# A prologue of layer norm and weight splitting, put in another order

## The chip, the core and the metric

The kernel runs on one core of a Trainium2 chip. The metric is the device time of one execution, in microseconds. Lower is better. The median of three runs of the kernel before is 1116.12 us (1115.36 to 1117.17).

## The reference

One transformer layer: cross attention, then a feed-forward network with quantised operands. Cut to what matters here, with shapes:

```python
# x (32, 100, 256), ctx (32, 361, 256), WQ, WK, WV (16, 256, 64), WO (1024, 256)
xn = (x - mean(x)) / sqrt(var(x) + 1e-5)            # over the last axis
Qh = einsum('btd,hdk->bhtk', xn, WQ)                 # 16 heads of 64
Kh = einsum('btd,hdk->bhtk', ctx, WK); Vh = einsum('btd,hdv->bhtv', ctx, WV)
attn = softmax(Qh Kh^T / sqrt(64) + mask * -1e9)
x = x + concat(attn Vh) @ WO
y = (x - mean(x)) / sqrt(var(x) + 1e-5)
x = x + qlinear(gelu(qlinear(y, W1, b1)), W2, b2)    # affine 8-bit codes of the input, symmetric of the weight
```

## The kernel before, in words

The kernel is written engine by engine: each of the five engines has its own instruction list in program order, and semaphores alone connect them. Nothing reorders it. An instruction that waits holds up everything behind it on its engine.

Phase 1, where the change lies, makes the query projection for all 32 batch rows, before a loop over the 32 rows does the attention. It goes through `NB` = 8 chunks of `TB` = 4 batch rows, 400 tokens each (`TW`). For chunk c:

- SyncE loads x into `xs` (`load_x`, L480), and between the chunks the four weights WQ, WK, WV, WO (L477 and L490), all through one queue.
- VectorE takes `bn_stats` of the four rows (`stats_x`, L876). Mean and variance follow from the two halves of each statistic by eight small operations (`ln_moments`, L461 to L468), each waiting for the one before. VectorE does them for chunk 0, GpSimd for the others. GpSimd then computes `rstd` by a power (L566) and `shift` (L567).
- ScalarE writes the normalised `xn` (`norm_x`, L685), TensorE transposes it (`x_transposes`, L1183), ScalarE copies the transposes out as f16 `xnT_h` (`x_high`, L693), and VectorE subtracts to get the remainder `xnT_l` (`x_low`, L881). Every operand is thus a high and a low f16 part.
- A weight is split likewise. VectorE takes the absolute maximum per partition (`abs_w`, L839), TensorE transposes it (`top_w`, L1191), VectorE makes the unit and its inverse (`unit_w`, L845 to L849), ScalarE writes the high part (`high_w`, L677) and VectorE the low part (`low_w`, L869), each in two halves of 512 columns.
- TensorE multiplies (`q_chunk`, calling `split3`, L366 to L368): eight products m of 400 columns, each the sum over two halves k of the contraction of high x high, high x low and low x high. Even m go to the PSUM bank `proj[0]`, which ScalarE copies out (`q_out`, L697), odd m to `proj[1]`, which VectorE copies out (`q_out`, L886). In the middle of a chunk, before m = 4, TensorE transposes the next chunk.

In VectorE's order, work for later chunks and weights stands between the copies. Before the first copy, at L945 to L956, stand the statistics of chunks 0, 1 and 2 and the whole preparation of WQ. On ScalarE the normalisation of chunk 1 stands ahead of the first copy, and on TensorE the transposes of chunk 0 stand ahead of WQ's `top_w`.

Of the kernel before, what the change touches and what calls it, by code (L numbers as in the profile page):

```python
# [15 lines left out]
F32 = mybir.dt.float32  # L16
# [4 lines left out]
ALU = mybir.AluOpType  # L21
# [155 lines left out]
def build(nc, x, ctxT, mask, wq, wk, wv, wo, w1T, b1, w2T, b2, out):  # L177
# [5 lines left out]
    def place(name, shape, dt, at=None):  # L183
        size = {F32: 4, F32R: 4, BF16: 2, F16: 2}[dt]
        n = size
        for d in shape[1:]:
            n *= d
        if at is None:
            at = cursor[0]
            cursor[0] = (at + n + 31) // 32 * 32  # L190
            assert cursor[0] <= top, (name, cursor[0], top)
        return nc.alloc_sbuf_tensor_at(name, shape, dt, offset=at)
# [10 lines left out]
    stats = place("stats", [P, B, 6], F32)  # L203
    mean = place("mean", [P, B], F32)
    var = place("var", [P, B], F32)
    rstd = place("rstd", [P, B], F32)
    shift = place("shift", [P, B], F32)
    lnt = place("lnt", [P, 4, B], F32)
# [161 lines left out]
    def wait(eng, s, n):  # L370

        eng.wait_ge(s, n + CREDIT)
# [6 lines left out]
    def chain(eng, s):  # L379

        count = [0]

        def link(ins):
            count[0] += 1
            ins.then_inc(s, 1)
            eng.wait_ge(s, count[0])
        return link
# [157 lines left out]
    def _(pool):  # L545
# [12 lines left out]
        link = chain(pool, s_lp)  # L558
        for c in range(NB):
            bs = slice(c * TB, (c + 1) * TB)  # L560
            if c == 0:
                pool.wait_ge(s_lv, 8)
            else:
                pool.wait_ge(s_st, TB * (c + 1))
                ln_moments(link, pool, c)
            link(pool.tensor_tensor(rstd[0:T, bs], var[0:T, bs], mhalf[0:T, bs], ALU.pow))  # L566
            pool.tensor_tensor(shift[0:T, bs], mean[0:T, bs], rstd[0:T, bs], ALU.mult).then_inc(s_rs, 1)  # L567
# [103 lines left out]
    def _(act):  # L671
# [8 lines left out]
        def norm_x(c, par):  # L680

            act.wait_ge(s_rs, c + 1)
            for i in range(TB):
                b = c * TB + i
                ins = act.activation(xn[0:T, par, i, :], xs[0:T, b, :], ACT.Identity, scale=rstd[0:T, b:b + 1],  # L685
                                     bias=shift[0:T, b:b + 1])
            ins.then_inc(s_xn, 1)
# [7 lines left out]
        def q_out(c, m):  # L695
            act.wait_ge(s_qp, NM * c + m + 1)
            act.activation(q_slot[:, c * TB:(c + 1) * TB, m, :], proj[0][:, 0:TW].rearrange("p (b t) -> p b t", b=TB),  # L697
                           ACT.Copy, scale=QS).then_inc(s_qe[0], 1)

        def q_chunk(c, par, more=True):  # L700
            split = (c - 1 if 2 <= c <= 4 else None)
            q_out(c, 0)
            if split:
                high_w(split, 0)
            q_out(c, 2)
            if more:
                x_high(c + 1, 1 - par)
            q_out(c, 4)
            if c + 2 < NB:
                norm_x(c + 2, par)  # L710
            if c == NB - 2:
                act.wait_ge(s_msk, 16)
                act.activation(mask_b[0:T, 0:S], mask_b[0:T, 0:S], ACT.Copy, scale=-1.0e9).then_inc(s_mb, 1)
            if split:
                high_w(split, 1)
            q_out(c, 6)
# [1 line left out]
        x_high(0, 0)  # L718
        high_w(0, 0)
        high_w(0, 1)  # L720
        norm_x(1, 1)
        for c in range(NB - 1):
            if c == NB - 2:
                act.wait_ge(s_wlo, 8)
# [107 lines left out]
    def _(dve):  # L832
# [39 lines left out]
        def stats_x(c):  # L872

            dve.wait_ge(s_x[c], 16)
            for b in range(c * TB, (c + 1) * TB):
                dve.bn_stats(stats[0:T, b, :], xs[0:T, b, :]).then_inc(s_st, 1)  # L876
# [29 lines left out]
        def q_chunk(c, par, more=2):  # L906

            q_out(c, 1)
            if c < 3:
                abs_w(c + 1, 0)  # L910
            elif c < 6:
                low_w(c - 2, 0)
            else:
                abs_f(3 * (c - 6))
            q_out(c, 3)
            if more:
                x_low(c + 1, 1 - par)
            q_out(c, 5)
            if more == 2 and c + 3 < NB:
                stats_x(c + 3)  # L920
            if 1 <= c <= 3:
                unit_w(c)
            if c == 6:
                abs_f(1)
            if c == 7:
                unit_f()
            q_out(c, 7)
            if c < 3:
                abs_w(c + 1, 1)
            elif c < 6:  # L930
                low_w(c - 2, 1)
            elif c == 6:
                abs_f(2)
            if c == 4:
                ctx_max(0)
            if c == 5:
                wait(dve, s_ct, 1)
                ctx_top(0, tp[0])
                dve.scalar_tensor_tensor(out=wconst[:, 0:1], in0=wunit[:, 0:1], scalar=GS, in1=wunit[:, 1:2],
                                         op0=ALU.mult, op1=ALU.mult).then_inc(s_wc, 1)  # L940
                dve.wait_ge(s_wc, 1)
                ctx_unit(0)
                dve.scalar_tensor_tensor(out=wconst[:, 1:2], in0=wunit[:, 2:3], scalar=1.0 / VS, in1=wunit[:, 3:4],
                                         op0=ALU.mult, op1=ALU.mult).then_inc(s_wc, 1)
        stats_x(0)  # L945
        dve.wait_ge(s_st, TB)
        ln_moments(chain(dve, s_lv), dve, 0)
        stats_x(1)
        abs_w(0, 0)
        abs_w(0, 1)  # L950
        unit_w(0)
        low_w(0, 0)
        start(dve, (s_k, s_v, s_cm, s_cr, s_sv, s_max, s_mg, s_hv, s_ri, s_nrm, s_x1, s_ln))
        x_low(0, 0)
        low_w(0, 1)
        stats_x(2)  # L956
        for c in range(NB):
# [215 lines left out]
    def _(pe):  # L1173
# [28 lines left out]
        def top_ctx(a, ps):  # L1202
            wait(pe, s_cm, a + 1)
            pe.transpose(ps[:, 512 - P:512], cmax[:, 0:1].broadcast_to([P, P]), ident[:, :]).then_inc(s_ct, 1)

        def q_chunk(c, par, more=True):
            wait(pe, s_xtl, KD * (c + 1))
            for m in range(NM):
                if m == NM // 2 and more:
                    x_transposes(c + 1, 1 - par)  # L1210
                if m == NM // 2 and 1 <= c <= 3:
                    top_w(c)
                if m == NM // 2 and c == 5:
                    top_ctx(0, tp[0])
                if m == NM // 2 and c == NB - 1:
                    top_f()
                wait(pe, s_qe[m % 2], NM // 2 * c + m // 2)
                if c == 0 and m % (NM // 2) == 0:
                    pe.wait_ge(s_wlo, m // (NM // 2) + 1)
                for k in range(KD):  # L1220
                    ms = slice(m * P, (m + 1) * P)
                    ins = split3(pe, proj[m % 2][:, 0:TW], (wq_h[:, k, ms], wq_l[:, k, ms]),
                                 (xnT_h[:, par, k, :], xnT_l[:, par, k, :]), k == 0, k == KD - 1)
                ins.then_inc(s_qp, 1)
        x_transposes(0, 0)
        top_w(0)
        for c in range(NB):
            q_chunk(c, c % 2, c < NB - 1)

# [219 lines left out]
```

## Time and profile before

| | |
|---|---|
| median of three runs | 1116.12 us |
| the profiled execution | 1116.15 us |
| its span in the trace | 1114.3 us |
| TensorE matmul busy | 1026.3 us (92%) |
| VectorE busy | 982.0 us (88%) |
| ScalarE busy | 866.6 us (78%) |
| GpSimd busy | 770.5 us (69%) |

The span is what the trace covers, from the first instruction to the last, and the time of the execution holds 1.85 us more. Busy shares are averages over the whole program. In the first of forty slices (28 us each) TensorE is busy 4 tenths, and 9 tenths in nearly all others. In the rows below, PE is TensorE's matmuls, PEld its weight loads, DVE VectorE, ACT ScalarE, POOL GpSimd, and SPq SyncE's queue.

### The profile page before, as it was taken

How to read it: one execution, taken by the hardware profiler on the slowest of the kernel's cores; microseconds unless marked ns; L12 is line 12 of the kernel's file. 1: busy time of each engine (PE TensorE's matmuls, PEld its weight loads, DVE VectorE, ACT ScalarE, POOL GpSimd, SP SyncE). 2: the span in 40 equal slices, each digit the busy share in tenths (PEclk: the TensorE clock that was granted, in tenths of full speed). 3: DMA queues.
4: the chain of work that ended last, by engine and by line, in shares of the span. 5: the costliest groups of instructions: out<-in, count | busy, mean ns of one | idle time of the engine just before them, and what ended most of it. 6: DMA issues, size and time to landing. Idle time of an engine off the chain costs nothing.

```text
span 1114.3 us, 37739 instructions
## 1 busy us (share of the span) xinstructions
PE 1026.3 (92%) x10639; PEld 649.0 (58%) x10639; DVE 982.0 (88%) x2538; ACT 866.6 (78%) x1809; POOL 770.5 (69%) x1106
## 2 busy tenths in 40 slices
PE   4999999999999999999999999999999999998828
PEld 2555566666666666666666666666666666665317
DVE  5776999999999999999999999999999999996997
ACT  4555888888888888888888888888888888886906
POOL 2337777777777777777777777777777777774800
PEclk9999999999999999999999999999999999999969
DMA  8301665555555555555555555555555555554003
GB/s 260 109 1 29 130 131 136 136 132 132 131 129 135 136 136 136 134 129 133 136 133 129 134 132 129 135 136 129 128 135 136 135 131 129 132 136 143 1 0 119
DMA packets 435437, 136.77 MB, mean 123 GB/s; under 512 B 407666, under 2 KB 434390, under 8 KB 435414
## 3 DMA queue, kind: packets, MB, share of 16 engines
q1 hardware_dynamic: 435414, 136.47, 51.0%
q8 instruction: 13, 0.21, 0.1%
q14 instruction: 10, 0.08, 0.0%
HBM read 28.60 MB, written 6.55 MB: 32 GB/s over the span
## 4 chain that ended last, share of the span: by engine, by line
PE 75%; DVE 10%; ACT 6%; issue 4%; POOL 3%; DVEq 1%; DMA 1%; ACTq 1%; SPq 0%; POOLq 0%
PE front L366 19%; PE front L368 17%; PE front L367 17%; PE back L1300 8%; PE front L1278 6%; PE tp L1278 5%; POOL hl L610 3%; DVE hrange L1129 2%; DVE hrange L1130 2%; DVE prob L979 2%; ACT prob L736 2%; DVE k_l L1028 1%; ACT q_h L790 1%; ACT ctx_h L786 1%; PE front L1415 1%
## 5 line engine op out<-in xcount | busy, mean ns | idle before, releaser
L610 POOL TENSOR_TENSOR hl<-prob,hl 100x361 f16<-100x361 f32 x511 | 432.0, 855 | 96.6 <-DVE hl L986 50.7
L736 ACT ACTIVATE prob<-prob,nmax 100x361 f32<-100x361 f32 x512 | 293.8, 586 | 47.7 <-DVE nmax L979 47.6
L366 PE MATMUL front<-ctx_h,wk_h 128*128 128x362 f16 x512 | 164.2, 321 | 31.6 <-POOL ctx_l L599 18.0
L1300 PEld LDWEIGHTS back<-v,pT 128*128 128x128 f16 (+1 forms) x4608 | 163.9, 97 | 38.9 <-issue 9.6
L742 ACT ACTIVATE hl<-prob 100x361 f16<-100x361 f32 x352 | 176.1, 500 | 7.9
L1300 PE MATMUL back<-v,pT 128*128 128x65 f16 (+1 forms) x4608 | 172.8, 193 | 0.6 <-DMA pT<-hl 0.5
L368 PE MATMUL front<-ctx_h,wk_l 128*128 128x362 f16 x512 | 161.7, 316 | 0.0
L367 PE MATMUL front<-ctx_l,wk_h 128*128 128x362 f16 x512 | 161.5, 315 | 0.0
L746 ACT ACTIVATE k_h<-front 128x362 f16<-128x362 f32 x256 | 119.0, 465 | 54.6 <-PE front L368 54.6
L1028 DVE SCALAR_TENSOR_TENSOR k_l<-front,k_h 128x362 f16<-128x362 f32 x256 | 135.2, 528 | 24.3 <-ACT k_h L746 21.6
L979 DVE CUSTOM_DVE_ANT_0 prob<-front,mask_g,ngain 100x361 f32<-100x361 f32 x256 | 149.6, 585 | 2.3
L1034 DVE SCALAR_TENSOR_TENSOR v<-front,v 128x512 f16<-128x512 f32 (+1 forms) x192 | 132.9, 692 | 20.2 <-ACT v L750 17.1
L979 DVE CUSTOM_DVE_ANT_0 prob<-tp,mask_g,ngain 100x361 f32<-100x361 f32 x256 | 147.4, 585 | 3.1
L750 ACT ACTIVATE v<-front 128x512 f16<-128x512 f32 (+1 forms) x192 | 114.5, 597 | 45.6 <-PE front L368 41.5
L366 PE MATMUL front<-wv_h,ctx_h 128*128 128x512 f16 (+1 forms) x384 | 145.9, 380 | 0.0
L367 PE MATMUL front<-wv_l,ctx_h 128*128 128x512 f16 (+1 forms) x384 | 145.5, 379 | 0.0
L368 PE MATMUL front<-wv_h,ctx_l 128*128 128x512 f16 (+1 forms) x384 | 145.5, 379 | 0.0
L986 DVE CAST hl<-prob 100x361 f16<-100x361 f32 x160 | 131.8, 824 | 0.3 <-ACT prob L736 0.3
L614 POOL TENSOR_TENSOR ahl<-att,ahl 100x256 f16<-100x256 f32 x127 | 84.0, 672 | 28.0 <-ACT ahl L756 28.0
L366 PEld LDWEIGHTS front<-ctx_h,wk_h 128*128 128x128 f16 x512 | 49.6, 97 | 88.4 <-DVE k_l L1028 27.9
L599 POOL TENSOR_TENSOR ctx_l<-ctx_raw,ctx_h 128x361 f16<-128x361 f32 x64 | 53.2, 854 | 43.9 <-ACT ctx_h L786 43.9
L366 PE MATMUL front<-wo_h,attT 128*100 128x256 f16 x256 | 71.0, 277 | 1.3 <-ACT attT L766 0.7
(205 smaller groups left out, 2006.5 us busy)
## 6 DMA issues: line engine op xcount, KB each, us to landing
ctx_raw<-ctxT SPq DMA_DIRECT2D x33, 361.0 KB, 3.2
pT<-hl SPq DMA_TRANSPOSE x253, 3.1
xs<-x SPq DMA_DIRECT2D x8, 400.0 KB
q_all<-x SPq DMA_DIRECT2D x32, 100.0 KB
out<-q_all SPq DMA_DIRECT2D x32, 100.0 KB
xb<-out SPq DMA_DIRECT2D x5, 640.0 KB, 8.1
out<-xb SPq DMA_DIRECT2D x25, 128.0 KB, 1.8
q_all<-wq SPq DMA_DIRECT2D x1, 1024.0 KB, 6.3
```

Of the source, the lines that this page charges most:

```text
L366: eng.matmul(dst, lh, rh, start=first, stop=False)
L367: eng.matmul(dst, lh, rl, start=False, stop=False)
L368: return eng.matmul(dst, ll, rh, start=False, stop=final)
L610: pool.tensor_tensor(hl[0:T, n % RT, 1, 0:S], prob[0:T, n % RP, 0:S], hl[0:T, n % RT, 0, 0:S], ALU.subtract).then_inc(s_lo, 1)
L736: act.activation(prob[0:T, n % RP, 0:S], prob[0:T, n % RP, 0:S], ACT.Exp, bias=nmax[0:T, n:n + 1], scale=-1.0).then_inc(s_exp, 1)
L742: act.activation(hl[0:T, h % RT, 0, 0:S], prob[0:T, h % RP, 0:S], ACT.Copy).then_inc(s_ha, 1)
L979: dve.tensor_tensor_reduce(prob[0:T, n % RP, 0:S], ring[n % RP][0:T, 0:S], mask_g[0:T, 0:S], ngain[0:T, 0:1], 3.0e38, ALU.add, ALU.min, nm ...
L986: dve.tensor_copy(hl[0:T, h % RT, 0, 0:S], prob[0:T, h % RP, 0:S]).then_inc(s_hv, 1)
L1028: dve.scalar_tensor_tensor(out=k_l[:, n % 4, :], in0=ps[:, 0:SE], scalar=KS, in1=k_h[:, n % 4, :], op0=ALU.mult, op1=ALU.subtract).then_in ...
L1034: dve.scalar_tensor_tensor(out=v[:, 1], in0=ps[0:rows_of(n), :].rearrange("p (h d) -> p h d", h=HT), scalar=VS, in1=v[:, 0], op0=ALU.mult, ...
L1278: ins = pe.matmul(ring[(2 * n + h) % RP][:, 0:SE], qs[rows[h], n, :], ks[rows[h], n % 4, :], start=t == 0, stop=t == 2)
L1300: ins = pe.matmul(obank[j % 2][:, n % GH * DV:(n % GH + 1) * DV], pT[0:r, n % RT, part_ * ST + st, :], v2[half][0:r, st, v, n % HT, :], st ...
```

## The change

Four pieces, all ahead of or within chunk 0:

1. Chunks 0 and 1 get mean and variance by `bn_aggr` on VectorE (`pair_x`), one instruction per batch row, and two more for the form that GpSimd wants. GpSimd no longer does the eight small operations for chunk 1.
2. On VectorE, WQ's maximum, its unit, `x_low` of chunk 0 and the first half of the low part now stand ahead of the statistics of chunk 1. On ScalarE, `norm_x(1, 1)` stands behind the first output copy.
3. TensorE's first two products (m = 0 and 1) are issued by terms: all that need the high part of WQ, for both products, then all that need the low part.
4. TensorE has 120 small matmuls on the identity ahead of `top_w(0)` and 48 between the transposes of chunk 0 and the first product. Their output is read by nobody. `top_w(0)` now stands ahead of the transposes.

```diff
@@ -203,6 +203,7 @@
     stats = place("stats", [P, B, 6], F32)
     mean = place("mean", [P, B], F32)
     var = place("var", [P, B], F32)
+    pair = place("pair", [P, 2 * TB, 2], F32)
     rstd = place("rstd", [P, B], F32)
     shift = place("shift", [P, B], F32)
     lnt = place("lnt", [P, 4, B], F32)
@@ -558,8 +559,8 @@
         link = chain(pool, s_lp)
         for c in range(NB):
             bs = slice(c * TB, (c + 1) * TB)
-            if c == 0:
-                pool.wait_ge(s_lv, 8)
+            if c < 2:
+                pool.wait_ge(s_lv, (TB + 2) * (c + 1))
             else:
                 pool.wait_ge(s_st, TB * (c + 1))
                 ln_moments(link, pool, c)
@@ -700,6 +701,8 @@
         def q_chunk(c, par, more=True):
             split = (c - 1 if 2 <= c <= 4 else None)
             q_out(c, 0)
+            if c == 0:
+                norm_x(1, 1)
             if split:
                 high_w(split, 0)
             q_out(c, 2)
@@ -718,7 +721,6 @@
         x_high(0, 0)
         high_w(0, 0)
         high_w(0, 1)
-        norm_x(1, 1)
         for c in range(NB - 1):
             if c == NB - 2:
                 act.wait_ge(s_wlo, 8)
@@ -942,16 +944,25 @@
                 ctx_unit(0)
                 dve.scalar_tensor_tensor(out=wconst[:, 1:2], in0=wunit[:, 2:3], scalar=1.0 / VS, in1=wunit[:, 3:4],
                                          op0=ALU.mult, op1=ALU.mult).then_inc(s_wc, 1)
+        def pair_x(c):
+
+            bs = slice(c * TB, (c + 1) * TB)
+            dve.wait_ge(s_st, TB * (c + 1))
+            for b in range(c * TB, (c + 1) * TB):
+                dve.bn_aggr(pair[0:T, b, :], stats[0:T, b, :]).then_inc(s_lv, 1)
+            dve.wait_ge(s_lv, (TB + 2) * c + TB)
+            dve.tensor_scalar(var[0:T, bs], pair[0:T, bs, 1], EPS, None, ALU.add).then_inc(s_lv, 1)
+            dve.tensor_scalar(mean[0:T, bs], pair[0:T, bs, 0], -1.0, None, ALU.mult).then_inc(s_lv, 1)
         stats_x(0)
-        dve.wait_ge(s_st, TB)
-        ln_moments(chain(dve, s_lv), dve, 0)
-        stats_x(1)
+        pair_x(0)
         abs_w(0, 0)
         abs_w(0, 1)
         unit_w(0)
-        low_w(0, 0)
         start(dve, (s_k, s_v, s_cm, s_cr, s_sv, s_max, s_mg, s_hv, s_ri, s_nrm, s_x1, s_ln))
         x_low(0, 0)
+        low_w(0, 0)
+        stats_x(1)
+        pair_x(1)
         low_w(0, 1)
         stats_x(2)
         for c in range(NB):
@@ -1203,8 +1214,25 @@
             wait(pe, s_cm, a + 1)
             pe.transpose(ps[:, 512 - P:512], cmax[:, 0:1].broadcast_to([P, P]), ident[:, :]).then_inc(s_ct, 1)
 
+        def first_two():
+
+            pe.wait_ge(s_whi, 1)
+            for m in range(2):
+                for k in range(KD):
+                    for t, x_ in enumerate((xnT_h, xnT_l)):
+                        pe.matmul(proj[m][:, 0:TW], wq_h[:, k, m * P:(m + 1) * P], x_[:, 0, k, :],
+                                  start=k == 0 and t == 0, stop=False)
+            pe.wait_ge(s_wlo, 1)
+            for m in range(2):
+                for k in range(KD):
+                    ins = pe.matmul(proj[m][:, 0:TW], wq_l[:, k, m * P:(m + 1) * P], xnT_h[:, 0, k, :],
+                                    start=False, stop=k == KD - 1)
+                ins.then_inc(s_qp, 1)
+
         def q_chunk(c, par, more=True):
             wait(pe, s_xtl, KD * (c + 1))
+            if c == 0:
+                first_two()
             for m in range(NM):
                 if m == NM // 2 and more:
                     x_transposes(c + 1, 1 - par)
@@ -1215,15 +1243,26 @@
                 if m == NM // 2 and c == NB - 1:
                     top_f()
                 wait(pe, s_qe[m % 2], NM // 2 * c + m // 2)
-                if c == 0 and m % (NM // 2) == 0:
-                    pe.wait_ge(s_wlo, m // (NM // 2) + 1)
+                if c == 0 and m < 2:
+                    continue
+                if c == 0 and m == NM // 2:
+                    pe.wait_ge(s_wlo, 2)
                 for k in range(KD):
                     ms = slice(m * P, (m + 1) * P)
                     ins = split3(pe, proj[m % 2][:, 0:TW], (wq_h[:, k, ms], wq_l[:, k, ms]),
                                  (xnT_h[:, par, k, :], xnT_l[:, par, k, :]), k == 0, k == KD - 1)
                 ins.then_inc(s_qp, 1)
+        def warm_up(times):
+
+            for _ in range(times):
+                for h in range(2):
+                    pe.matmul(tp[1][h * DK:(h + 1) * DK, 0:T], identb[:, h * DK:(h + 1) * DK], identb[:, 0:T],
+                              start=True, stop=True)
+
+        warm_up(60)
+        top_w(0)
         x_transposes(0, 0)
-        top_w(0)
+        warm_up(24)
         for c in range(NB):
             q_chunk(c, c % 2, c < NB - 1)
 
```

VectorE before, from its start to its first output copy (statistics `stats`, moments `mean` and `var`, WQ's maxima `wabs`, remainders `wq_l` and `xnT_l`; the last row is the copy into `q_all`):

```order
L876 BN_STATS stats<-xs 100x6 x3
L461 TENSOR_TENSOR lnt<-stats 100x4 [waits s_st]
...
L468 TENSOR_TENSOR var<-lnt 100x4 [waits s_lv]
L876 BN_STATS stats<-xs 100x6 [waits s_xin1,s_lv]
...
L839 TENSOR_REDUCE wabs<-q_all 128x1 [waits s_wraw0]
...
L849 RECIPROCAL winv<-wunit 128x1 [waits s_wr]
L869 SCALAR_TENSOR_TENSOR wq_l<-q_all,winv,wq_h 128x2x512 [waits s_whi]
L881 TENSOR_TENSOR xnT_l<-front,xnT_h 128x400 [waits s_xth] x2
L869 SCALAR_TENSOR_TENSOR wq_l<-q_all,winv,wq_h 128x2x512 [waits s_whi]
L876 BN_STATS stats<-xs 100x6 [waits s_xin2]
...
L886 TENSOR_SCALAR q_all<-front 128x4x100 [waits s_qp]
```

The same stretch of VectorE now:

```order
L952 BN_AGGR pair<-stats 100x2 [waits s_st]
...
L954 TENSOR_SCALAR var<-pair 100x4 [waits s_lv]
...
L841 TENSOR_REDUCE wabs<-q_all 128x1 [waits s_wraw0]
...
L851 RECIPROCAL winv<-wunit 128x1 [waits s_wr]
L883 TENSOR_TENSOR xnT_l<-front,xnT_h 128x400 [waits s_xth] x2
L871 SCALAR_TENSOR_TENSOR wq_l<-q_all,winv,wq_h 128x2x512 [waits s_whi]
L878 BN_STATS stats<-xs 100x6 [waits s_xin1]
...
L952 BN_AGGR pair<-stats 100x2 x3
...
L955 TENSOR_SCALAR mean<-pair 100x4
L871 SCALAR_TENSOR_TENSOR wq_l<-q_all,winv,wq_h 128x2x512 [waits s_whi]
L878 BN_STATS stats<-xs 100x6 [waits s_xin2]
...
L888 TENSOR_SCALAR q_all<-front 128x4x100 [waits s_qp]
```

The wait for chunk 1 of x (`s_xin1`) has moved from ahead of WQ's maximum to behind `x_low` and the first low half, together with the statistics and aggregates of chunk 1.

TensorE before, from its start into the second product:

```order
L1183 MATMUL front<-ident,xn 128x100 [waits s_xtl,s_xn,s_id]
L1183 MATMUL front<-ident,xn 128x100 x7
L1191 MATMUL tp<-ident,wabs 128x128 [waits s_wa]
L1191 MATMUL tp<-ident,wabs 128x128
L366 MATMUL front<-xnT_h,wq_h 128x400 [waits s_wlo,s_qe0,s_xtl]
L367 MATMUL front<-xnT_l,wq_h 128x400
L368 MATMUL front<-xnT_h,wq_l 128x400
```

TensorE now, from its start to the fourth product:

```order
L1259 MATMUL tp<-identb 64x100 x119
L1202 MATMUL tp<-ident,wabs 128x128 [waits s_wa]
...
L1194 MATMUL front<-ident,xn 128x100 [waits s_xtl,s_xn]
L1194 MATMUL front<-ident,xn 128x100 x7
L1259 MATMUL tp<-identb 64x100 x48
L1223 MATMUL front<-xnT_h,wq_h 128x400 [waits s_whi,s_xtl]
L1223 MATMUL front<-xnT_l,wq_h 128x400
...
L1228 MATMUL front<-xnT_h,wq_l 128x400 [waits s_wlo]
L1228 MATMUL front<-xnT_h,wq_l 128x400 x3
L367 MATMUL front<-xnT_h,wq_h 128x400 [waits s_qe0,s_qe1]
...
L367 MATMUL front<-xnT_h,wq_h 128x400 [waits s_qe1]
```

The maximum's transposes have moved ahead of those of x, the small matmuls stand on both sides, and the first product waits for the high part (`s_whi`) where it waited for the low part (`s_wlo`).

## Rows read from the trace of the kernel before

**Rows 1.** Chain of waits, 0 to 35 us: start us, us, what
```profile
1.70 8.39 DMA xs<-x
...
18.95 0.52 PE front L366
...
20.47 0.33 PE front L367
...
24.43 0.17 PE front L367
```

**Rows 2.** Table by stretch, 40 to 50 us: busy time and (instructions) of each engine
```profile
core 0: us, PE busy (x) PEld busy (x) DVE busy (x) ACT busy (x) POOL busy (x), PEclk, DMA share, GB/s
40.00:50.00 10.00, 8.97 (x58) 5.46 (x57) 8.14 (x16) 6.72 (x12) 3.25 (x14) 1.00 0.01 2
```

**Rows 3.** Timeline, 0 to 26 us: start us, us, engine, line, op [idle before]
```profile
1.68 0.29 POOL L553 TENSOR_SCALAR_AFFINE_SELECT identb<-identb 128x128 f16<-128x128 f16 x1
...
6.35 0.17 DVE L461 TENSOR_TENSOR lnt<-stats 100x4 f32<-100x4 f32 x1
...
7.76 0.16 DVE L468 TENSOR_TENSOR var<-lnt 100x4 f32<-100x4 f32 x1
...
8.01 1.04 POOL L566 TENSOR_TENSOR rstd<-var,mhalf 100x4 f32<-100x4 f32 x1 [5.95 <-DVE var L468]
...
9.13 0.20 POOL L567 TENSOR_TENSOR shift<-mean,rstd 100x4 f32<-100x4 f32 x1
9.37 2.07 ACT L685 ACTIVATE xn<-xs,shift,rstd 100x256 f32<-100x256 f32 x4 [7.29 <-POOL shift L567]
...
11.51 2.33 DVE L839 TENSOR_REDUCE wabs<-q_all 128x1 f32<-128x1024 f32 x2
...
13.89 0.69 PE L1191 MATMUL tp<-ident,wabs 128*128 128x128 f32 x2 [0.79 <-DVE wabs L839]
...
15.27 0.17 DVE L849 RECIPROCAL winv<-wunit 128x1 f32<-128x1 f32 x1
15.47 2.19 ACT L677 ACTIVATE wq_h<-q_all,winv 128x1024 f16<-128x1024 f32 x2 [1.82 <-DVE winv L849]
16.65 1.28 DVE L869 SCALAR_TENSOR_TENSOR wq_l<-q_all,winv,wq_h 128x1024 f16<-128x1024 f32 x1 [1.22 <-ACT wq_h L677]
...
17.85 1.05 DVE L881 TENSOR_TENSOR xnT_l<-front,xnT_h 128x400 f16<-128x400 f32 x2
...
20.01 1.40 DVE L876 BATCH_NORM_STATS2 stats<-xs 100x6 f32<-100x256 f32 x4
...
22.77 0.58 DVE L886 TENSOR_SCALAR q_all<-front 128x400 f32<-128x400 f32 x1 [1.37 <-PE front L368]
...
24.60 0.85 PE L1183 MATMUL front<-ident,xn 100*128 100x100 f32 x8
...
24.84 0.20 POOL L567 TENSOR_TENSOR shift<-mean,rstd 100x4 f32<-100x4 f32 x1
25.15 0.90 ACT L693 ACTIVATE xnT_h<-front 128x400 f16<-128x400 f32 x2 [0.86 <-PE front L1183]
...
25.29 0.34 PE L366 MATMUL front<-xnT_h,wq_h 128*128 128x400 f16 x1
```

**Rows 4.** DMA issues: out<-in, queue, op, count, KB each, us to landing
```profile
q_all<-wq SPq DMA_DIRECT2D x1, 1024.0 KB, 6.3
q_all<-wk SPq DMA_DIRECT2D x1, 1024.0 KB, 12.6
```

**Rows 5.** Timeline of TensorE at 602 us, in the attention loop
```profile
602.48 0.99 PE L1300 MATMUL back<-v,pT 128*128 128x65 f16 x27
```

**Rows 6.** TensorE's timeline and the granted clock, 1056.9 to 1080 us
```profile
1056.99 1.76 PE L1397 MATMUL front<-yT,w1q 128*128 128x400 f16 x8
...
1063.00:1064.00 1.00, 0.00 (x0) 0.00 (x0) 1.00 (x2) 0.00 (x0) 0.00 (x0) 0.63 0.00 0
...
1077.27 2.96 PE L1367 MATMUL tp<-w1q 128*128 128x256 f16 x13 [18.52 <-DVE hrange L1130]
```

## The prediction

> **What bounds the kernel now.** The chain of waits comes first, because the change touches only the prologue and the question is whether the prologue lies on the path that sets the end. It does: the chain begins with SyncE's issues and the wait for chunk 1 of x, whose landing releases VectorE at 10.09 [rows 1], and from there every step to the first product at 18.95 is one of the moved instructions. After it the chain is matmul after matmul, 0.33 us apart and later 0.17 us [rows 1]. The table by stretch then says what follows: in 40 to 50 us TensorE is busy 8.97 of 10 us, VectorE 8.14 and ScalarE 6.72 [rows 2]. So phase 1 is paced by TensorE with short turnarounds, and the engines wait for each other, not for the clock on the wall. A shift of chunk 0 is passed on whole if no transfer is late. The profiled execution took 1116.15 us, 1114.3 of them span; the median of the runs is 1116.12, so one base serves for both.
>
> The timeline of the first 26 us [rows 3] shows two waits worth reading. VectorE finishes the moments of chunk 0 at 7.92 and then waits, because chunk 1's statistics stand ahead of WQ's maximum, although WQ lands 6.3 us after an issue at 1.21 [rows 4], so at 7.5, or 7.95 if counted from the issue's end. And TensorE starts cold: 400 columns take 0.333 us, which is 1.2 GHz, and from about 22.1 on 0.17, which is 2.4 GHz [rows 1]. The granted clock column reads 1.00 in both stretches, so here I read the level from the spacing.
>
> **Moments of chunk 0.** Removed: eight small VectorE operations with a wait each, from 6.35 to 7.92, 1.57 us [rows 3]. Added: four aggregates without waits between them, a wait, and two operations of 100x4. The trace has no aggregate. From below, an aggregate adds nothing beside the chained ones (0); from above each costs a chained step, 0.20 us. I take 0.11 each, midway, since they are queued without waits: 0.45, then 0.05 + 0.17 + about 0.1 for the last two. They end at 7.1 (6.7 to 7.5). GpSimd then needs 1.04 + 0.08 + 0.20 for rstd and shift, as before 8.01 to 9.33, and ScalarE 2.07 for the four xn [rows 3]: xn is ready at 10.6 instead of 11.44.
>
> **WQ's maximum first.** It starts at the later of VectorE free (7.1) and WQ landed (7.5 to 7.95); I take 7.75. Two reductions take 2.33, to 10.1 instead of 13.84 [rows 3]. From the maximum's transposes at 13.89 to the end of winv at 15.44 is 1.55 us before [rows 3]; with TensorE warm the transposes shrink from about 0.7 to 0.45, so winv stands at 11.4. The order on TensorE is turned round (top_w, then x_transposes): xn at 10.6 meets it free. Warm, the first evacuation of transposes begins 0.55 after they do (24.60 to 25.15) and the pair takes 0.90 [rows 3]: ScalarE copies 11.2 to 12.1. Now its queue, not winv, is last: wq_h half 0 runs 12.1 to 13.25, half 1 to 14.3 (2.19 for the pair [rows 3]).
>
> **First two products by terms.** The eight matmuls on wq_h need the first half only and start at 13.25, or when the second warm-up run ends (below, 13.6): 8 x 0.167 = 1.35, to 14.9. VectorE does x_low, 1.05, to 12.8, then wq_l half 0, 13.3 to 14.6 (1.28 [rows 3]). The four matmuls on wq_l end the two products at 15.6. Before, the twelve ran from 18.95, about ten of them 0.333 apart, and VectorE's copy of the second began at 22.77 [rows 3]. That is 7 us earlier. But it isn't what is gained.
>
> **What is late next.** Behind x_low VectorE now has, ahead of its first output copy: wq_l half 0 to 14.6; statistics of chunk 1, 1.40, to 16.0; their aggregates, 0.8, to 16.8; wq_l half 1, 1.28, to 18.1; statistics of chunk 2, 1.40, to 19.5. Each is a duration of [rows 3]. The copy that frees the second bank thus starts at 19.45, while its product has been ready since 15.6; before it started at 22.77 straight on its product. TensorE does m=2 when ScalarE's copy has ended (15.5 to 16.0), 16.05 to 17.1, and then waits for the second bank until 20.05. The gain here is 22.77 - 19.45 = 3.3 us.
> ScalarE meanwhile reaches norm_x(1) behind its first copy; shift of chunk 1 is ready at 16.8 + 1.35 = 18.15, the norms end at 20.25 (2.07), and ScalarE's second copy at 20.7. Both precede their readers: TensorE ends m=3 at 21.05, transposes chunk 1 to 21.75 and starts m=4 at 21.7, against 25.29 [rows 3]. So 3.3 by the second bank and 3.6 at m=4: I take 3.4. GpSimd no longer does the eight moments of chunk 1, so chunk 2's begin at 19.55 and end with shift at 23.1 (3.6 us, as 21.48 to 25.04, whose last operation stands in [rows 3]); norm_x(2), behind the copy of m=4, wants them at about 23.4. Just covered. WK lands 12.6 after an issue from 2.61 to 4.60 [rows 4], at 17.2 at the latest; its reader now comes at 19.95. Later readers keep far more distance.
>
> **The warm-up runs.** 120 matmuls of 100 columns on 64-column halves, from the identity's end at 1.97 [rows 3]. Cold, streaming costs 0.333 / 4 = 0.083. The start at 18.95 is cold for 3.1 us, and so, with 13 matmuls of 256 columns in the first 2.96 us, is the run at 1077.27 [rows 6]. So about 38 cold ones to 5.1 and 82 at 0.042 to 0.055: the run ends at 8.6 to 9.6, before top_w's 10.1, costing nothing. No row shows 64-column halves. From below, the two halves run side by side: end at 6 to 7, and TensorE idles until 10.1. From above, loading isn't hidden: 0.083 + twice the 0.037 of a small matmul in [rows 5] (0.99 / 27) = 0.157 cold and 0.079 warm: 20 in 3.1 us, 100 in 7.9, an end at 13.0. The second run, 48 from 11.45, ends at 13.6 by 0.044 (12.5 to 15.2 by the ends); its excess is absorbed, as VectorE's queue sets the next step.
> On this a page bears. The 27 matmuls of [rows 5] have 128-column weights and take 37 ns each, so their loads, too, cost at most that in a run. The Trainium skill (TensorE: Matmul & The Clock Gate, Weight-path perf modes) says that fast weight load is on only with 128 weights, and its page TensorEngine Tiling (Array Packing), Restrictions, that column tiling disables it. By that rule the halves load at the slow rate, which speaks for the upper end; by the 27 matmuls, for the lower.
>
> **Rivals.**
> *The clock falls in TensorE's new gap* (17.1 to 20.05, about 3 us). In the trace the clock fell about 4.5 us after the last matmul ended at 1058.75: the slice 1063 to 1064 shows 0.63 [rows 6]. 3 us is less, which speaks against it. If it falls, about 3.1 us of matmuls run at half rate and lose 1.55: 1116.15 - 1.9 = 1114.3. The Trainium skill (TensorE: Matmul & The Clock Gate, Why this matters for your kernels) warns against idle stretches between bursts of matmuls; by its rule this rival's time holds.
> *The warm-up is longer than its cover, but the clock rises*: at the upper end, 13.0, top_w is 2.9 late, everything behind it too, and the gain is 0.5: 1115.6; at half of that excess it is 1.9: 1114.2. Of the same size: chunk 2's moments or a transfer late, so that the shift is partly given back.
> *Slower: the warm-up never warms and blocks.* Half-width matmuls on an identity might not raise the clock. At 0.157 each they end at 20.8; top_w is 10.7 late, cold transposes and products add 0.9: 1116.15 - 3.4 + 11.6 = 1124.3. It decides from the point where top_w is 3.4 - 0.9 = 2.5 late, an end at 12.6, 0.088 each cold; at the streaming rate of 0.083 it would still be a gain of 0.6. Against it: every dense run in the trace rose.
> *It doesn't matter*: the shift is lost in a wait on something fixed, say a transfer; 1116.1. The DMA queue is full until 39 us, but each landing has its distance.
>
> **How the numbers follow.** Forecast, gain 2.9 to 4.0 around 3.4: 0.65, giving 1112.7. Clock falls: 0.12. Warm-up too long or partly given back: 0.12. Nothing: 0.06. Slower: 0.05. More than expected has no case of its own beyond 4.0, apart from the scatter of the median (before: 1115.36 to 1117.17). About 0.2%, 2.2 us, is what can be told from no change, so faster means under 1113.9: the forecast, and a bit of the others, 0.68; same 0.27; slower 0.05. The range 1111.4 to 1115.2 holds the forecast and most of the two middle cases.
>
> **What would show it.** VectorE's first WQ reduction at 7.5 to 8.0; winv by 11.4; first product's matmuls at 13.3 to 14, 0.17 apart; VectorE without idle from 13.3 to 20; its first output copy at 19.5 (this is the sum's main term); m=4 at 21.7; from there on every phase 1 row 3.4 earlier than before, to the loop. Wrong, if top_w waits for the warm-up, if m=3 steps at 0.33, or if norm_x(2) waits for shift.

## The result and the profile after

| | before | changed |
|---|---|---|
| median | 1116.30 us (17 runs, 1115.36 to 1117.17) | 1113.67 us (17 runs, 1112.80 to 1114.46) |
| ratio, 95% interval | | 0.9977 [0.9969, 0.9984] |
| profiled execution, span | 1116.15, 1114.3 | 1113.10, 1111.2 |

The change is worth 2.6 us; 1112.7 was forecast, within 1111.4 to 1115.2. Ten of the seventeen times of the changed kernel lie between 1112.80 and 1113.77, the other seven between 1114.14 and 1114.46; the profiled one is of the lower part, and no trace shows what the upper seven did. The forecast's gain was 3.4, and the profiled pair shows 3.05, of which phase 1 holds 2.5. ScalarE's first copy of a K product, the first work behind phase 1, marks its end; below, first from the kernel before, then from the changed kernel (start us, us, engine, line, op [idle before]):

```profile
98.14 0.47 ACT L746 ACTIVATE k_h<-front 128x362 f16<-128x362 f32 x1 [0.60 <-PE front L368]
```
```profile
95.65 0.47 ACT L748 ACTIVATE k_h<-front 128x362 f16<-128x362 f32 x1 [0.60 <-PE front L369]
```

I call this start the K mark. In all fourteen profiles, those of the experiments included, the time of the execution stands 1017.2 to 1018.0 us above its K mark. So the differences arise ahead of the K mark, and what lies behind it only scatters by some 0.8 us. The changed kernel's timeline from 2 to 23 us, lines that answer to [rows 3]:

```profile
2.03 4.82 PE L1259 MATMUL tp<-identb 128*64 128x100 f16 x120 [2.03 <-POOL identb L554]
...
6.84 0.38 DVE L952 BATCH_NORM_AGGREGATE pair<-stats 100x2 f32<-100x6 f32 x4
...
8.22 2.34 DVE L841 TENSOR_REDUCE wabs<-q_all 128x1 f32<-128x1024 f32 x2 [0.73 <-DMA q_all<-wq]
...
10.63 0.69 PE L1202 MATMUL tp<-ident,wabs 128*128 128x128 f32 x2 [3.78 <-DVE wabs L841]
...
12.02 0.50 ACT L694 ACTIVATE xnT_h<-front 128x400 f16<-128x400 f32 x1 [1.02 <-PE front L1194]
12.58 2.21 PE L1259 MATMUL tp<-identb 128*64 128x100 f16 x48
...
13.09 2.18 ACT L678 ACTIVATE wq_h<-q_all,winv 128x1024 f16<-128x1024 f32 x2
...
14.26 1.28 DVE L871 SCALAR_TENSOR_TENSOR wq_l<-q_all,winv,wq_h 128x1024 f16<-128x1024 f32 x1
...
14.72 0.51 PE L1223 MATMUL front<-xnT_h,wq_h 128*128 128x400 f16 x1
...
15.03 0.54 PE L1223 MATMUL front<-xnT_l,wq_h 128*128 128x400 f16 x1
...
17.46 1.28 DVE L871 SCALAR_TENSOR_TENSOR wq_l<-q_all,winv,wq_h 128x1024 f16<-128x1024 f32 x1
...
17.63 1.99 POOL L567 TENSOR_TENSOR rstd<-var,mhalf 100x4 f32<-100x4 f32 x1 [8.73 <-DVE mean L955]
...
19.93 2.07 ACT L686 ACTIVATE xn<-xs,shift,rstd 100x256 f32<-100x256 f32 x4 [1.94 <-POOL shift L568]
19.97 0.56 DVE L888 TENSOR_SCALAR q_all<-front 128x400 f32<-128x400 f32 x1
...
20.59 0.34 PE L367 MATMUL front<-xnT_h,wq_h 128*128 128x400 f16 x1 [1.28 <-DVE q_all L888]
...
22.06 0.72 PEld L1194 LDWEIGHTS front<-ident,xn 100*128 100x128 f32 x8 [0.68 <-ACT xn L686]
...
22.80 0.33 PE L367 MATMUL front<-xnT_h,wq_h 128*128 128x400 f16 x1
```

VectorE no longer waits for chunk 1's statistics, and its first copy has come from 22.77 to 19.97. But the transposes of chunk 1 wait for ScalarE's norm, that for GpSimd's shift, and GpSimd's power lasts 1.99 us where it took 1.04. The product m = 4 starts at 22.80, 2.49 earlier than the 25.29 of [rows 3], and the K mark has moved by the same 2.49. The chain of waits of the changed kernel runs over these very steps (start us, us, what):

```profile
14.26 1.28 DVE wq_l L871
...
16.90 0.39 DVE pair L952 x4
...
17.63 2.00 POOL rstd L567
19.70 0.21 POOL shift L568
19.93 2.08 ACT xn L686 x4
22.06 0.91 PE front L1194 x8
```

The table by stretch tells of the clock, the number behind POOL's (columns as in [rows 2]):

```profile
9.00:10.00 1.00, 0.00 (x0) 0.00 (x0) 1.00 (x2) 1.00 (x3) 0.00 (x0) 0.84 0.98 219
10.00:11.00 1.00, 0.37 (x2) 0.29 (x2) 0.57 (x1) 1.00 (x3) 0.00 (x0) 0.50 1.07 245
...
16.00:17.00 1.00, 1.00 (x6) 0.55 (x5) 0.97 (x5) 0.00 (x0) 0.00 (x0) 0.75 1.07 274
```

It fell to 1.2 GHz (called cold here, and 2.4 GHz warm) at about 9.7, in TensorE's idle stretch from 6.85 to 10.63, and rose again about 16.5. The maximum's transposes, those of chunk 0, the second warm-up run and six of the first eight matmuls were cold.

### The profile page after: what moved, and what is told of

Same layout as the page of the kernel before. It is cut to its first block, busy times and chain, and to the rows that moved or that the text cites. A ratio compares the mean times of both kernels' runs of the same rounds, so it can differ in the third digit from the quotient of the medians.

```text
span 1111.2 us, 38071 instructions
## 1 busy us (share of the span) xinstructions
PE 1033.0 (93%) x10807; PEld 655.4 (59%) x10807; DVE 981.5 (88%) x2542; ACT 866.2 (78%) x1809; POOL 768.5 (69%) x1098
## 4 chain that ended last, share of the span: by engine, by line
PE 74%; DVE 10%; ACT 6%; issue 4%; POOL 3%; DMA 1%; DVEq 1%; ACTq 1%; POOLq 0%; SPq 0%
PE front L367 19%; PE front L369 16%; PE front L368 16%; PE back L1339 8%; PE front L1317 6%; PE tp L1317 5%; POOL hl L611 3%; DVE hrange L1140 2%; DVE hrange L1141 2%; ACT prob L738 2%; DVE prob L990 2%; DVE k_l L1039 1%; ACT q_h L792 1%; ACT ctx_h L788 1%; PE front L1454 1%
## 5 line engine op out<-in xcount | busy, mean ns | idle before, releaser
L1039 DVE SCALAR_TENSOR_TENSOR k_l<-front,k_h 128x362 f16<-128x362 f32 x256 | 135.2, 528 | 24.4 <-ACT k_h L748 21.7
```

Source lines behind the costliest of these rows:

```text
L1039: dve.scalar_tensor_tensor(out=k_l[:, n % 4, :], in0=ps[:, 0:SE], scalar=KS, in1=k_h[:, n % 4, :], op0=ALU.mult, op1=ALU.subtract).then_in ...
```

## The experiments

All ratios are to runs of the kernel before on the same chip. The last three columns are of one profiled execution each. Where its time is far from the median, its K mark doesn't speak for the run: the profiled executions of wq_second, fill and before_again_b were the slowest of theirs, by 1.2, 1.6 and 1.2 us above the median.

| run | median, ratio to before [95%] | profiled | m = 4 starts | K mark |
|---|---|---|---|---|
| changed | 1113.67, 0.9977 [0.9969, 0.9984] | 1113.10 | 22.80 | 95.65 |
| no_warm | 1113.31, 0.9970 [0.9958, 0.9981] | 1113.91 | 23.04 | 95.89 |
| warm_full | 1113.20, 0.9970 [0.9958, 0.9982] | 1113.59 | 22.74 | 95.59 |
| warm_long | 1114.62, 0.9983 [0.9974, 0.9992] | 1113.84 | 23.41 | 96.46 |
| no_terms_b | 1112.91, 0.9973 [0.9963, 0.9982] | 1112.85 | 22.59 | 95.44 |
| wq_second | 1116.38, 0.9996 [0.9987, 1.0005] | 1117.53 | 26.90 | 99.74 |
| norm_early | 1117.63, 1.0012 [1.0002, 1.0021] | 1116.58 | 26.50 | 99.34 |
| no_aggr | 1117.87, 1.0012 [1.0003, 1.0021] | 1117.30 | 25.50 | 99.89 |
| port | 1114.88, 0.9984 [0.9975, 0.9993] | 1114.52 | 23.59 | 96.90 |
| port2_b | 1111.95, 0.9963 [0.9949, 0.9977] | 1111.94 | 21.77 | 94.61 |
| fill | 1112.83, 0.9970 [0.9959, 0.9981] | 1114.41 | 23.87 | 96.94 |
| fill2_b | 1111.67, 0.9960 [0.9946, 0.9973] | 1111.91 | 21.35 | 94.20 |
| before_again_b | 1116.20, 0.9999 [0.9989, 1.0010] | 1117.38 | 26.62 | 99.49 |

**The small matmuls, left out (no_warm).**

```diff
-        warm_up(60)
         top_w(0)
         x_transposes(0, 0)
-        warm_up(24)
```

> The changed kernel without its 168 small matmuls. Theory (VectorE's queue, then GpSimd's power and the norm of chunk 1, set m = 4; the small matmuls set nothing): the first product starts at 14.3 instead of 14.72, all twelve matmuls of the first two products are cold and end about 18.5, m = 2 follows ScalarE's copy at about 18.4, VectorE's first copy stays at 20.0 and m = 4 at 22.8; time 2.5 below the kernel before, as the changed kernel. Rival (the warm clock is worth something): m = 4 later than 23.2, the gain under 2.1.

Measured: as the theory. The first output copy on VectorE came at 20.21, m = 4 at 23.04, and the interval of the ratio contains the changed kernel's ratio. The 168 matmuls bring nothing that can be told here.

**Longer, and over the whole array (warm_long, warm_full).**

```diff
-        warm_up(60)
+        warm_up(116)
# warm_full, besides: one matmul for each pair
+                pe.matmul(tp[1][:, 0:T], identb[:, :], identb[:, 0:T], start=True, stop=True)
```

> First run of small matmuls 116 pairs instead of 60. Theory (pairs run side by side, the clock rises about 6.0 us and fell at 9.7 because TensorE stood idle from 6.85 to 10.63): 48 pairs by 6.0, 68 at about 0.06 to 10.1; the clock stays at 2.4 GHz, top_w and the transposes of chunk 0 are warm, ScalarE's first copy comes 0.6 earlier (11.4) and with it everything on VectorE; m = 4 at 22.2, gain 3.1 over the kernel before. Rival (pairs never raise the clock): they run 0.083 each to 11.7, top_w is 1.1 late, m = 4 at 23.9 or later, gain 1.4.

> The small matmuls over all 128 columns of the array, one in place of each pair, 116 and 24 of them. Theory: 0.083 each until the clock rises at about 6.0, then 0.042 to 0.045, end at 9.1, the gap to 10.6 is too short for the clock to fall; as with the longer run of pairs, m = 4 at 22.2 and gain 3.1. Rival (no rise): end at 11.7 and m = 4 at 23.9.

Measured: both keep the clock up over top_w, whose transposes take 0.43 instead of 0.69, and from the start of WQ's first reduction to that of wq_h passes 4.24 us in warm_full against 4.87 in the changed kernel. So the warm clock is worth 0.6 there. But m = 4 came at 22.74 in warm_full and at 23.41 in warm_long, not at 22.2. In warm_full 0.35 of the 0.6 is eaten by WQ's later landing (8.57 instead of 8.22), and most of the rest by something that the expectation left out: VectorE's twelve semaphore increments (`start` in the diff of the change), which now stand between winv and x_low and take 0.98 us.

```profile
12.09 0.16 DVE L851 RECIPROCAL winv<-wunit 128x1 f32<-128x1 f32 x1
...
12.81 2.19 ACT L678 ACTIVATE wq_h<-q_all,winv 128x1024 f16<-128x1024 f32 x2
13.23 1.06 DVE L883 TENSOR_TENSOR xnT_l<-front,xnT_h 128x400 f16<-128x400 f32 x2 [0.98 <-ACT xnT_h L694]
14.21 1.27 DVE L871 SCALAR_TENSOR_TENSOR wq_l<-q_all,winv,wq_h 128x1024 f16<-128x1024 f32 x1
```

The row names ScalarE's copy, but 0.98 or 0.99 us stand behind winv in every variant with this order (1.09 in no_aggr), and warm_long's chain of waits goes through the twelve increments, 11.84 to 12.95. Where VectorE waits for half 0 of wq_h, as in no_warm, it gets it 1.17 us after ScalarE's start (13.33 to 14.50). By that it was there at 13.98 in warm_full and 13.45 in warm_long, while wq_l began at 14.21 and 13.93, behind x_low. In the changed kernel the two come together (14.26), so there the increments cost nothing. In warm_long, besides, TensorE stood 1.02 us without cause in the trace between small matmuls, and its faster first products left a gap of 2.45 us before m = 3; the clock fell 0.2 us after that gap, and the transposes of chunk 1 took 1.54 instead of 0.91. The times can't tell a gain of 3.1 from one of 2.6: warm_full's is 3.4, with an interval from 2.0 to 4.7.

**The first two products in the old order (no_terms).**

```diff
-            if c == 0:
-                first_two()
-                if c == 0 and m < 2:
-                    continue
-                if c == 0 and m == NM // 2:
-                    pe.wait_ge(s_wlo, 2)
+                if c == 0 and m % (NM // 2) == 0:
+                    pe.wait_ge(s_wlo, m // (NM // 2) + 1)
```

> One part undone: the first two products are issued in the old order, waiting for the first low half. Theory (the first two products are not on the path, because VectorE copies m = 1 only at 20.0): m = 0 runs from 15.6 to 17.3, m = 1 to 18.3, m = 3 at 20.6 and m = 4 at 22.8 stay, gain 2.5 as changed. Rival (terms are worth their 2 us): m = 4 at 23.5 or later, gain 1.8 or less.

Measured: as the theory; 22.59, and 0.9973. Issuing by terms brings nothing that can be told.

**WQ's maximum behind chunk 1 again (wq_second).**

```diff
         pair_x(0)
+        stats_x(1)
+        pair_x(1)
         abs_w(0, 0)
...
         low_w(0, 0)
-        stats_x(1)
-        pair_x(1)
```

> One part undone: on VectorE statistics and aggregates of chunk 1 stand ahead of WQ's maximum again, all else as changed. Theory (what counts is when x_low and the low halves come): the maximum starts at 12.3 instead of 8.2, winv at 16.2, VectorE's first copy at 22.0, xn of chunk 1 is bound by ScalarE's queue and ends at 23.7, m = 4 at 24.5 against 22.80 as changed and 25.29 before: gain 0.8. Rival (the path through shift of chunk 1 is what counts, and that is early here): m = 4 at or before 22.8, gain 2.5 or more.

Measured: the direction of the theory, but m = 4 came 2.4 later than it forecast, and 1.6 later than before. Statistics waited for x of chunk 1 until 12.08, WQ's maximum began at 14.08, and the first copy came at 23.87. In the kernel before x of chunk 1 released the statistics at 10.19; this later landing, 1.9 us, is not part of the edit. By the medians, 1116.38 against 1116.32 of before, this part carries the whole gain; the 4.1 us of K mark are of the slowest execution.

**The norm of chunk 1 ahead of the first copy again (norm_early).**

```diff
-            if c == 0:
-                norm_x(1, 1)
...
         high_w(0, 1)
+        norm_x(1, 1)
```

> One part undone: the normalisation of chunk 1 stands ahead of ScalarE's first copy again. Theory: ScalarE waits for shift of chunk 1 until 19.9, normalises to 22.0 and only then copies m = 0; TensorE stands idle from 17.8 to 22.5, which is enough for its clock to fall; m = 4 at 25.2 with a warm clock, about 26.7 with a cold one: time between 0.1 below and 1.5 above the kernel before. Rival (ScalarE's order does not matter, VectorE's copy of m = 1 is last): m = 4 at 22.8, gain 2.5.

Measured: the theory with the cold clock, 26.50, and 1.3 us slower than before by the medians. The stretch from 20 to 22 us shows a mean granted clock of 0.94 (it fell at about 21.8), the next one 0.50:

```profile
20.00:22.00 2.00, 0.00 (x0) 0.00 (x0) 1.59 (x2) 2.00 (x5) 1.41 (x7) 0.94 0.64 218
22.00:24.00 2.00, 1.52 (x5) 0.72 (x6) 0.00 (x0) 0.33 (x1) 1.41 (x3) 0.50 0.68 200
```

**The eight small operations again (no_aggr).**

```diff
-        pair_x(0)
+        dve.wait_ge(s_st, TB)
+        ln_moments(chain(dve, s_lv), dve, 0)
...
-        pair_x(1)
# and GpSimd takes chunk 1 by ln_moments, waiting for the statistics alone
```

> One part undone: moments of chunks 0 and 1 by the eight small operations again, chunk 0 on VectorE and chunk 1 on GpSimd. Theory: xn of chunk 0 is 0.9 late and with it everything on VectorE; GpSimd starts chunk 1's moments at 17.8, is held up beside the second low half for 1.2 us, shift of chunk 1 ends at 22.6, norm at 24.7, m = 4 at 25.5, later if the clock falls in the long gap: time 0 to 1.5 above the kernel before. Rival (moments are off the path, the low halves are on it): m = 4 at 23.7, gain 1.6.

Measured: m = 4 at 25.50, as said, and then the clock fell while TensorE worked (0.93 in 24 to 26, 0.50 in 26 to 28), so that the K mark is 4.2 later than the changed kernel's. Without the aggregates the other parts bring a loss of 0.12%. In the profile most of that loss is the fall of the clock: m = 4 is 0.2 later than before, the K mark 1.75.

**GpSimd and the subtraction (port, port2).** In port only the two last lines change places; port2 also puts the first copy between.

```diff
         pair_x(1)
-        low_w(0, 1)
         stats_x(2)
+        q_out(0, 1)     # port2 only
+        low_w(0, 1)
```

> VectorE takes the statistics of chunk 2 ahead of the second low half of WQ, so that GpSimd's power for chunk 1 does not run beside the f32 subtraction. Theory (the subtraction holds GpSimd up): the power takes 1.04 instead of 1.99, shift of chunk 1 ends at 18.9, norm_x(1) at 21.0, m = 4 starts after m = 3 and eight transposes at 22.3 instead of 22.80, gain 3.0 over the kernel before. Rival (the power was slow for another reason, such as transfers into SBUF): it stays near 2.0, m = 4 stays at 22.8.

> Changed kernel with VectorE's order: statistics and aggregates of chunk 1, statistics of chunk 2, first output copy, and only then the second low half of WQ. Theory (GpSimd stands still as long as an f32 subtraction from SBUF runs on VectorE): rstd and shift of chunk 1 run 17.6 to 18.9 undisturbed, norm_x(1) ends at 21.0, VectorE's first copy comes at 18.9, m = 3 at 19.5, m = 4 at 21.7 against 22.80, and TensorE's gap shrinks below 1.5 us, so its clock stays: gain 3.6 over the kernel before. Rival (the clock falls in the gap in any case, or m = 4 waits for the low half): m = 4 at 22.6 or later, gain 2.7 or less.

Measured in port: rstd took 1.02, as the theory says, but shift, 0.20 us of work, was caught by the subtraction in its place (timeline of GpSimd and VectorE):

```profile
18.68 1.37 POOL L568 TENSOR_TENSOR shift<-mean,rstd 100x4 f32<-100x4 f32 x1
18.72 1.27 DVE L871 SCALAR_TENSOR_TENSOR wq_l<-q_all,winv,wq_h 128x1024 f16<-128x1024 f32 x1
```

It ends 0.06 us after the subtraction, so xn of chunk 1 came no earlier. And the clock fell at about 21.1, as m = 3 ran at last behind a gap of 2.3 us, so the transposes of chunk 1 took 1.59 instead of 0.91, and m = 4 came at 23.59, later than both readings had it:

```profile
21.00:22.00 1.00, 1.00 (x5) 0.25 (x2) 0.60 (x1) 1.00 (x3) 0.67 (x4) 0.55 0.64 197
```

In port2 both operations run free, 17.56 to 18.86, and the copy comes at 18.70 (the subtraction, now at 19.18, holds up a small operation of chunk 2 instead, 1.08 us from 19.43):

```profile
17.56 1.02 POOL L567 TENSOR_TENSOR rstd<-var,mhalf 100x4 f32<-100x4 f32 x1 [8.66 <-DVE mean L956]
18.66 0.20 POOL L568 TENSOR_TENSOR shift<-mean,rstd 100x4 f32<-100x4 f32 x1
18.70 0.56 DVE L888 TENSOR_SCALAR q_all<-front 128x400 f32<-128x400 f32 x1
```

m = 4 at 21.77, as forecast (21.7), and 1.0 us of K mark gained over the changed kernel. That this equals what GpSimd had stood still is no proof: the edit does two things at once, it frees GpSimd and brings VectorE's first copy 1.27 us forward, and no run has one without the other.

**Filling VectorE's waits (fill, fill2).** fill2's order of VectorE, with norm_x(1) in its old place on ScalarE:

```diff
         abs_w(0, 1)
+        start(dve, ...)
         unit_w(0)         # fill: stats_x(1), unit_w(0), start, pair_x(1)
-        start(dve, ...)
+        stats_x(1)
+        pair_x(1)
         x_low(0, 0)
         low_w(0, 0)
-        stats_x(1)
-        pair_x(1)
         low_w(0, 1)
+        q_out(0, 1)
         stats_x(2)
+        pair_x(2)
```

Both take the aggregates for chunk 2 as well (`pair_x(2)`).

> Built on the changed kernel: statistics of chunk 1 in VectorE's wait for the transposes of WQ's maximum, its aggregates behind winv, both low halves together, the first output copy ahead of the statistics of chunk 2, aggregates for chunk 2 as well, and norm_x(1) back ahead of ScalarE's first copy, where ScalarE stood idle. Theory: shift of chunk 1 by 15, norm_x(1) 15.6 to 17.7, VectorE's first copy at 17.8, m = 3 at 19.2, m = 4 at 20.9: gain 4.4 over the kernel before, and no gap of TensorE over 0.7 us after 14.7. Rival (a transfer or chunk 2's moments become the bound): gain 3.4 or less, with norm_x(2) waiting for shift, or the statistics of chunk 1 or 2 waiting for x.

> As the earlier run fill, with statistics of chunk 1 behind winv, so that WQ's unit does not wait for x of chunk 1, and the twelve semaphore increments ahead of it. Theory: WQ's high part at 13.1, statistics of chunk 1 at its landing near 12.2 to 13.6, x_low 14.1 to 15.2, both low halves to 17.6, first copy 17.6, norm_x(1) 15.3 to 17.4, m = 3 at 19.0, m = 4 at 20.8: gain 4.2 to 4.5 over the kernel before. Rival (transfers have become the bound: x of chunk 1 and WK): gain 3.5 or less, with VectorE waiting for a DMA ahead of the statistics of chunk 1 or of WK's maximum.

Measured: fill missed. Its median is 3.5 us below before, against 4.4. Statistics of chunk 1 waited for x until 12.32, and the unit of WQ stood behind them; 0.98 us more went into the twelve semaphore increments ahead of the aggregates. In the profiled execution, 1.6 us above the median, the clock moreover fell at 17.3 under the first products and came back at about 20.7; at half rate that costs about 1.7 us (an estimate), so m = 4 at 23.87 is hardly that of the median execution. fill2 moves both, and reaches m = 4 at 21.35 and 1111.67 us, the best here, 0.9960 of before. Its gain by m = 4 is 3.9, under the 4.2 forecast, since shift was again caught by a subtraction (1.03 us) and ScalarE's norm began at 16.03. Its distance to port2 is within the intervals.

**The kernel before, once more (before_again).** No edit.

> The kernel before, profiled a second time, to see when x of chunk 1 lands: 10.09 in the first profile, 12.08 and 12.3 in two changed kernels that wait for it. Theory A (the landing scatters from run to run, or between chips): it lands anywhere from 10 to 12.4 here, and the first K copy of the loop, 98.14 in the first profile, moves with it. Theory B (something in the change delays it, such as the instructions that TensorE fetches): it lands at 10.1 again.

Measured: the landing as theory B has it, 10.31 against the first profile's 10.19, but the K mark is 1.35 later, for a reason that neither theory names. TensorE's cold start lasted from 19.08 to about 24.7, not 3.1 us:

```profile
19.08 0.52 PE L366 MATMUL front<-xnT_h,wq_h 128*128 128x400 f16 x1 [4.37 <-DVE xnT_l L881]
...
24.39 0.52 PE L367 MATMUL front<-xnT_l,wq_h 128*128 128x400 f16 x1
24.72 0.36 PE L368 MATMUL front<-xnT_h,wq_l 128*128 128x400 f16 x1
24.91 0.33 PE L366 MATMUL front<-xnT_h,wq_h 128*128 128x400 f16 x1
```

The 2.5 us more at half the rate are 1.25 of the 1.35. So two executions of the kernel before differ by more than 1 us by their cold start. The profile that the prediction was made on was no lucky one: its 1116.15 is near the median of its runs, while this one, 1117.38, is the slowest of all runs of this kernel on its chip.

## Why the prediction was right, and where it was off

The mechanism was right: WQ's maximum first, VectorE's queue as the next bound of its first copy, the gap before m = 3, the pass of the whole shift through phase 1 (2.49 at m = 4, 2.49 at the K mark), and no gain from the early first products, which no_terms and no_warm confirm. Two terms of the sum were mis-sized; in part smaller ones offset them. Of the times named as signs only VectorE's full queue from 13.3 to 20 came as said; WQ's first reduction began at 8.22 (said: 7.5 to 8.0), winv was there at 12.15 (said: 11.4), the first product at 14.72 and 0.33 apart (13.3 to 14, 0.17 apart), the first copy at 19.97 (19.5) and m = 4 at 22.80 (21.7).

- *"With TensorE warm."* The sum took the transposes of the maximum and of chunk 0 at the warm price. The lower end of the warm-up term, pairs side by side and TensorE idle until 10.1, was what happened (120 in 4.82 us, an end at 6.85), but I had priced that end at nothing. The upper end, loads that aren't hidden at 0.157 us a matmul, is ruled out: each took 0.04. The clock fell about 2.8 us after the run's end. ScalarE's wq_h began at 13.09 instead of 12.1; 0.47 of that is WQ's landing (8.22 instead of 7.75), the rest, 0.5, the clock, as warm_full's 0.6 bears out.
- *"Shift of chunk 1 is ready at 18.15."* It ended at 19.90. The aggregates came 0.75 late by the points above; the other microsecond is GpSimd's power at 1.99 instead of 1.04, beside wq_l half 1. In the sum the norms ended 0.8 before m = 3 did; here they came last: TensorE stood 0.28 us for xn behind m = 3. In changed, no_warm, warm_full, no_terms and port2, m = 4 starts 2.90 or 2.91 after the end of shift. So the bank that VectorE's copy frees, the sum's main term, was worth 2.8 (22.77 to 19.97) and not what m = 4 waited for. How much of the missing 1.1 at m = 4 is GpSimd's is an estimate: with the power at 1.04, m = 3 would have been last, its six matmuls from 20.59 to 21.61, then 0.69 for the transposes as in [rows 3] (24.60 to 25.29), 22.3. That is 0.5 for GpSimd and 0.6 for VectorE's queue, which the cold clock and WQ's landing had made late. port2 takes both away (1.03 at m = 4).
- The trace of before already showed what such a neighbour costs, outside [rows 3]. Four small GpSimd operations of phase 1, elsewhere 0.20 us, began there beside the same kind of subtraction, and each ends 0.05 or 0.06 us after it. Two of them:

```profile
59.22 1.28 DVE L869 SCALAR_TENSOR_TENSOR wk_l<-q_all,winv,wk_h 128x1024 f16<-128x1024 f32 x1
59.33 1.22 POOL L465 TENSOR_TENSOR lnt<-lnt 100x4 f32<-100x4 f32 x1
...
61.47 1.02 POOL L566 TENSOR_TENSOR rstd<-var,mhalf 100x4 f32<-100x4 f32 x1
...
61.97 1.28 DVE L869 SCALAR_TENSOR_TENSOR wv_l<-q_all,winv,wv_h 128x1024 f16<-128x1024 f32 x1
62.57 0.73 POOL L567 TENSOR_TENSOR shift<-mean,rstd 100x4 f32<-100x4 f32 x1
```

  The Trainium skill (SBUF — State Buffer, SBUF: two separate sides) says that VectorE and GpSimd share a port pair as an exclusive lock, held for the whole instruction, also by a VectorE instruction with two SBUF inputs where the GpSimd one reads SBUF. The held-up operations agree as far as GpSimd's waiting goes (rstd 1.99 in six profiles, shift 1.37, 1.03 and 1.03, small additions 1.17 in no_aggr and 1.08 in port2, and these four in every profile), and in phase 1 none of GpSimd's operations on 100x4 was held up beside anything else that VectorE did. The other direction isn't borne out: above, the power began 0.5 us ahead of the subtraction, and both kept their usual 1.02 and 1.28; in port, shift began 0.04 ahead and was held all the same.
- Smaller than charged: four aggregates took 0.38, not 0.45, and the whole moments 0.65 from 6.84 to 7.49, against 0.8.
- Not charged at all: the twelve semaphore increments that the change moved. Before, they ran beside half 0 of wq_l (16.80 to 17.84 in before_again's chain of waits); now they stand between winv and x_low, 0.98 us. It is luck that this cost nothing in the changed kernel; with the warm clock that the sum assumed it costs 0.2 to 0.5, as warm_full and warm_long show.
- The rival that the clock falls in the gap before m = 3 got 0.12 on the reading that 3 us is less than the 4.5 of [rows 6]. In the changed kernel the gap was only 1.3 us, because cold first products and m = 2 filled it. That was luck too: with the warm first products of warm_long it was 2.45 us, and the clock fell just behind it. Gaps of 0.9 to 1.7 us before m = 3 passed without a fall (port2, changed, no_aggr, no_terms, warm_full), those of 2.3 (port) and 2.45 us (warm_long) did not, nor did 2.6 us before no_aggr's transposes of chunk 1 and 5.5 us before m = 2 in norm_early. After the first run of small matmuls the clock fell between 2.0 us (norm_early) and 5.3 us (no_terms, where TensorE had worked again for 1.0 us) after their end. One interval was no bound; the rival deserved about 0.3.

Not settled: in the changed variants x of chunk 0 releases VectorE at 5.1 to 5.8, in both profiles of before at 4.91 and 4.93; WQ lands 6.5 to 7.3 us after its issue against 6.2 and 6.3; x of chunk 1 releases the statistics at 12.1 and 12.3 in two variants (in fill2 it was there by 11.7), in before at 10.2 and 10.3. no_warm shows it too (5.64, 7.0), so the small matmuls aren't the cause. One thing that all variants share is the tile `pair`, which shifts every later tile in SBUF by 64 bytes or more. Whether that is it wasn't tried. Against the forecast's 7.75 WQ's later landing costs about 0.5 us of the gain.

## What to carry to other kernels

When a wait is taken off the front, write out the queue behind it on every engine and price each small operation by what its neighbour does at that moment, not by its lonely duration; a GpSimd step of 1.04 us took 1.99 beside a VectorE subtraction of two SBUF operands, and one of 0.20 us up to 1.37. Look for such a pair in the whole trace, not only in the stretch that changes. Count semaphore increments, too, when they move from beside a long operation to behind a short one. The warm-up matmuls could be left out here: keeping TensorE's clock up was worth 0.6 us at the one step where it shows, and later waits took that back. A part's price depends on the others: three of the parts, each undone alone, cost the whole gain.

## What the runs showed of the hardware that I had not expected

- Two matmuls on 64-column halves of the array run as one: 60 pairs of 100 columns in 4.82 us, 0.08 us a pair, as long as a full-width one of 100 columns takes cold: in 3 to 4 us the trace has 30 of the halves here, and 15 full-width ones in warm_full.
- TensorE's cold start lasted 3.1 us in one execution and 5.6 in another of the same kernel, on uninterrupted matmuls of 400 columns.
- The clock can fall while TensorE works again: in no_aggr it fell at about 25.7, although the transposes had begun at 24.75, and in warm_full at about 12.5, with TensorE at work since 10.97.
